# Attention products in four column tiles, denominators from ones, y moved by DMA instead of transposed

## The reference, cut to what matters

```
x = x + 0.5 * ffn0(ln(x));  x = x + attn0(ln(x));  x = x + 0.5 * ffn0(ln(x))
x = x + 0.5 * ffn1(ln(x));  x = x + attn1(ln(x));  x = x + 0.5 * ffn1(ln(x))
# attention: 2 batches, 1024 positions, 512 channels, 16 heads of 32; a0 has 4 key/value heads
att = softmax(where(causal, q k^T / sqrt(32), -inf));  y = att v;  out = y Wo
```

## Time and profile before

| | us |
|---|---|
| median of 3 runs | 2689.49 (2688.24 to 2693.65) |
| the profiled execution | 2691.6 |
| its span, first to last instruction | 2689.9 |
| PE busy | 2610.5 |
| VectorE busy | 1366.2 |
| ScalarE busy | 1081.1 |
| GpSimd busy | 638.1 |

### The profile page before, as it was taken

How to read it: one execution, slowest core, us unless ns; L and a number is a source line. 1 busy time by engine, 2 the same in 40 slices (tenths; PEclk the granted TensorE clock), 3 DMA queues, 4 the chain that set the end, 5 groups by cost and what they waited for, 6 DMA issues and landing times.

```text
span 2689.9 us, 36139 instructions
## 1 busy us (share of the span) xinstructions
PE 2610.5 (97%) x13216; PEld 1994.4 (74%) x13216; DVE 1366.2 (51%) x2784; ACT 1081.1 (40%) x1989; POOL 638.1 (24%) x1102
## 2 busy tenths in 40 slices
PE   6999999999999999999999999999999999999999
PEld 4788765666558888888888888666766678888887
DVE  7787566756655445433333344566366553333333
ACT  7555355655663223311121133666456631111121
POOL 3333532332223335311111130222122321111110
PEclk9999999999999999999999999999999999999999
DMA  4222121122120110100000002332122100000001
GB/s 145 71 71 75 52 52 33 37 56 49 39 86 1 36 44 9 39 25 24 24 24 24 24 24 58 78 80 60 37 66 68 42 24 28 28 24 24 24 16 63
DMA packets 59679, 119.80 MB, mean 45 GB/s; under 512 B 11632, under 2 KB 12656, under 8 KB 59504
## 3 DMA queue, kind: packets, MB, share of 16 engines
q1 hardware_dynamic: 59504, 117.51, 15.4%
HBM read 62.42 MB, written 13.63 MB: 28 GB/s over the span
## 4 chain that ended last, share of the span: by engine, by line
PE 84%; DVE 2%; ACT 2%; issue 2%; DMA 2%; POOL 1%; SPq 1%; DVEq 0%; ACTq 0%; POOLq 0%
PE psum L970 63%; PE psum L1091 9%; PE psum L1055 5%; PE psum L1073 4%; PE psum L979 1%; DMA raw<-in_o 1%; SPq L1644 1%; PE psum L1101 1%; PE psum L1111 1%; ACT s1a0e L1265 0%; ACT s4a1e L1265 0%; POOL rstd L1531 0%; POOL wmem L1543 0%; DVE s4a1masked L1440 0%; DMA raw<-in_q 0%
## 5 line engine op out<-in xcount | busy, mean ns | idle before, releaser
L970 PE MATMUL psum<-hA_hi,wmem 128*128 128x256 f32 (+1 forms) x1536 | 405.4, 334 | 0.1
L970 PE MATMUL psum<-hA_lo,wmem 128*128 128x512 f32 (+1 forms) x864 | 293.7, 340 | 0.0
L970 PEld LDWEIGHTS psum<-hA_hi,wmem 128*128 128x128 f32 x1536 | 270.0, 190 | 30.9 <-DVE wmem L1345 0.5
L1265 ACT ACTIVATE s4a1e<-psum,p_scale 128x384 f32<-128x384 f32 (+5 forms) x384 | 205.4, 581 | 99.1 <-PE psum L1073 96.7
L1265 ACT ACTIVATE s1a0e<-psum,p_scale 128x384 f32<-128x384 f32 (+5 forms) x384 | 205.1, 579 | 95.4 <-PE psum L1073 93.4
L1440 DVE CUSTOM_DVE_ANT_0 s4a1masked<-psum,mask_q 128x512 bf16<-128x512 f32 (+7 forms) x256 | 190.0, 751 | 90.3 <-PE psum L1055 89.1
L1392 DVE SCALAR_TENSOR_TENSOR x<-psum,x 128x512 f32<-128x512 f32 x256 | 175.6, 689 | 97.7 <-PE psum L970 93.4
L1440 DVE CUSTOM_DVE_ANT_0 s1a0masked<-psum,mask_q 128x512 bf16<-128x512 f32 (+7 forms) x256 | 189.1, 751 | 62.5 <-PE psum L1055 59.9
L1363 DVE TENSOR_TENSOR s5f1prod<-psum,s5f1silu 128x512 f32<-128x512 f32 x64 | 44.2, 691 | 314.5 <-PE psum L970 314.5
L1363 DVE TENSOR_TENSOR s3f1prod<-psum,s3f1silu 128x512 f32<-128x512 f32 x64 | 44.2, 691 | 294.5 <-PE psum L970 294.5
L970 PE MATMUL psum<-s3f1w,s3f1a 128*128 128x512 f32 x768 | 181.8, 391 | 0.9 <-POOL s3f1w L1543 0.9
(11 more groups left out here) (196 smaller groups left out, 5054.7 us busy)
## 6 DMA issues: line engine op xcount, KB each, us to landing
s1a0qst<-s1a0qs SPq DMA_DIRECT2D x96, 128.0 KB, 2.4
s4a1qst<-s4a1qs SPq DMA_DIRECT2D x96, 128.0 KB, 2.4
s4a1kst<-s4a1ks SPq DMA_DIRECT2D x96, 128.0 KB, 2.4
raw<-in_gate SPq DMA_DIRECT2D x44, 256.0 KB, 2.8
raw<-in_up SPq DMA_DIRECT2D x44, 256.0 KB, 2.7
raw<-in_down SPq DMA_DIRECT2D x44, 256.0 KB, 2.8
rounded<-s0f0w SPq DMA_DIRECT2D x24, 256.0 KB, 2.0
s2f0w<-rounded SPq DMA_DIRECT2D x24, 256.0 KB, 5.1
```

What stands on the lines that cost most here:

```text
L970: ins = pe.matmul(out_, w, m, start=n == 0, stop=n == len(terms) - 1)
L1265: act.activation(T[s]["e32"][:, begin_ + z * pw:begin_ + (z + 1) * pw - skip], src, ACT.Exp, bias=p_scale[:]).then_inc(sem["exp"], 1)
```

## The change

- `pv` cuts the queries of each 128-block in four quarters of 32 (QUAD = 256 columns per quarter) and sends them to four column tiles of 32 partitions. The value block is 32 columns, without the ones. Columns 0 to 255 of the bank hold y^T of a head.
- After each odd unit GpSimd adds the exponentials of the odd key block onto those of the even one in place (`e_add`). `den` multiplies this sum with a block of ones, in the same four tiles, to columns 256 to 511, so the denominator stands in all 32 rows of a quarter. As the even block now holds the sum, the odd value block is replaced by its difference from the even one (`v_out` on VectorE, `v_dif`).
- `y_fin` takes the reciprocal of 128 x 256 denominators and multiplies the 128 x 256 of y^T with it into `ysb`; `take`, `y_turn` and `y_tp` are gone. Four DMAs per head (`y_move`) bring the four quarters to the head's 32 partitions of `y`; `y_hi` and `y_lo` split the 1024 columns into high and low parts once per group.
- `piece_out` and `oproj` are cut in two steps each (`piece_lo`, `x_sum`), the second one step later. `row` writes the masked scores over the scores in PSUM; `masked` is gone. PV_LAG becomes 9, `e32` 7680 columns, and some steps start at other units.

```diff
-PV_LAG = 7
+PIECES_AT = 2
+Y_AT = 1
+Y_WAIT = 2
+YT_AT = 2
+O_LAG = 1
+NORMS_FROM = 11
+STACKS_AT = (18, 20, 26, 31)
+PV_LAG = 9
-E32 = 5632
+E32 = 7680
...
         def times_v(n, jt):
+            k = jt // 2
             plan.append(("pv", s, n, jt))
-            if jt == ST - 1:
-                job = [[], [("take", s, n)], [], [], [("y_turn", s, n)], [("y_fin", s, n)]]
+            if jt % 2 == 0:
+                plan.append(("den", s, n, k))
+                return
+            if k == PAIRS - 1:
+                job = [[]] * Y_AT + [[("y_fin", s, n)]] + [[]] * Y_WAIT + [[("y_move", s, n)]]
                 g, j = divmod(n, HPG)
                 if j == HPG - 1:
-                    job += [[("y_tp", s, g, 0)], [("y_tp", s, g, 1)], []]
-                    job += [[("oproj", s, g, t)] for t in range(ST)]
+                    job += [[]] * YT_AT + [[("y_hi", s, g)]] + [[("y_lo", s, g)]] + [[]] * O_LAG
+                    job += [[("oproj", s, g, t)] + [("x_sum", s, g, t - 1)] * (t > 0)
+                            for t in range(ST)] + [[("x_sum", s, g, ST - 1)]]
...
             plan.append(("e_mask", s, n, i))
+            if i % 2:
+                plan.append(("e_add", s, n, i // 2))
...
-                on.wait_ge(sem["exp"], at("exp", "key", s, n, jt, pieces - 1))
-                on.wait_ge(sem["e_mask"], at("e_mask", "e_mask", s, n, jt))
-                for c in range(2):
-                    ins = pe.matmul(psum[c * HALF:c * HALF + VW, bank, jt * HALF:CH],
+                name = ("v_out", "v_dif")[jt % 2]
+                on.wait_ge(sem[name], at(name, "v_out", s, n // HEADS, v_of(s, jt)))
+                on.wait_ge(sem["e_add"], at("e_add", "e_add", s, n, jt // 2))
+                for c in range(HPG):
+                    ins = pe.matmul(psum[c * HD:(c + 1) * HD, bank, jt * HD:QUAD],
                                     v[:, jt, kv, :], e[:, :, c, :], start=jt == 0,
                                     stop=jt == ST - 1, skip_group_check=True)
...
+            def den(s, n, k):
+                bank = banks["pv", s, n, 0][0]
+                on.wait_ge(const, CONSTS)
+                on.wait_ge(sem["e_add"], at("e_add", "e_add", s, n, k))
+                e = quarters(s, n, 2 * k)
+                for c in range(HPG):
+                    ins = pe.matmul(psum[c * HD:(c + 1) * HD, bank, QUAD + 2 * k * HD:CH],
+                                    ones[:], e[:, :, c, :], start=False,
+                                    stop=k == PAIRS - 1, skip_group_check=True)
+                ins.then_inc(sem["den"], 1)
...
             def y_fin(s, n):
+                bank, rden = banks["pv", s, n, 0][0], T[s]["rden"][n % 2]
+                on.wait_ge(sem["pv"], at("pv", "pv", s, n, ST - 1))
+                dve.reciprocal(rden[:], psum[:, bank, QUAD:CH]).then_inc(sem["y_rec"], 1)
+                if n >= 2:
+                    on.wait_ge(*y_moved(s, n - 2))
                 on.wait_ge(sem["y_rec"], at("y_rec", "y_fin", s, n))
+                dve.tensor_tensor(T[s]["ysb"][n % 2][:], psum[:, bank, 0:QUAD], rden[:],
                                   ALU.mult).then_inc(sem["y_fin"], 1)
...
+            def e_add(s, n, k):
+                begin, end = e32_place[s, n, 2 * k]
+                more, more_end = e32_place[s, n, 2 * k + 1]
+                _, _, pieces, _ = key_cols(2 * k + 1)
+                e32 = T[s]["e32"]
+                on.wait_ge(sem["exp"], at("exp", "key", s, n, 2 * k + 1, pieces - 1))
+                on.wait_ge(sem["e_mask"], at("e_mask", "e_mask", s, n, 2 * k + 1))
+                pool.tensor_tensor(e32[:, begin + P:end], e32[:, begin + P:end],
+                                   e32[:, more:more_end], ALU.add).then_inc(sem["e_add"], 1)
...
+            def y_move(s, n):
+                g, j = divmod(n, HPG)
+                on.wait_ge(sem["y_fin"], at("y_fin", "y_fin", s, n))
+                if g:
+                    on.wait_ge(sem["y_lo"], at("y_lo", "y_lo", s, g - 1))
+                for c in range(HPG):
+                    sp.dma_start(T[s]["y"][j * HD:(j + 1) * HD, c * QUAD:(c + 1) * QUAD],
+                                 T[s]["ysb"][n % 2][c * HD:(c + 1) * HD, :]
+                                 ).then_inc(moved[n % 2], 16)
```

More of the change, by code:

```diff
@@ L376 @@
     "gu": ("gate", "up", "silu", "prod", "a_hi"), "a_lo": ("a_lo",),
-    "k_ones": ("k_ones",), "v_ones": ("v_ones",),
+    "k_ones": ("k_ones",),
     "piece": ("proj",), "v_tile": ("v_mm",), "v_chunk": ("v_mm", "v_bias"), "v_turn": ("v_tp",),
-    "v_out": ("v_out",), "bias_x": ("x_pool",),
+    "bias_x": ("x_pool",),
     "row": ("s_q", "row_max"), "m_tp": ("m_tp", "m_hi"), "m_lo": ("m_lo",),
-    "key": ("s_k", "exp"), "e_mask": ("e_mask",), "pv": ("pv",), "take": ("y_take",), "y_turn": ("y_turn",),
-    "y_fin": ("y_rec", "y_fin"),
-    "y_tp": ("y_tp", "y_hi", "y_lo"), "oproj": ("o_proj", "x_add"),
+    "key": ("s_k", "exp"), "e_mask": ("e_mask",), "pv": ("pv",),
+    "e_add": ("e_add",), "den": ("den",), "y_fin": ("y_rec", "y_fin"),
+    "y_hi": ("y_hi",), "y_lo": ("y_lo",), "oproj": ("o_proj",), "x_sum": ("x_add",),
 }
@@ L419 @@
 FIT = 1
-EMPTIED_BY = {"piece": "piece_out", "v_tile": "v_out", "v_turn": "v_out", "m_tp": "m_lo",
-              "y_turn": "y_fin", "ln_tp": "ln_lo"}
+EMPTIED_BY = {"piece": "piece_lo", "oproj": "x_sum", "v_tile": "v_out", "v_turn": "v_out", "m_tp": "m_lo",
+              "ln_tp": "ln_lo"}
 def banks_wanted(step):
@@ L567, in bank_turns @@
             if step[0] == "pv":
-                release["take", step[1], step[2]] = mine
+                release["y_fin", step[1], step[2]] = mine
             elif step[0] in EMPTIED_BY:
@@ L917, in read_by @@
                 return sem["m_lo"], at("m_lo", "m_lo", *step[1:])
-            name = {"gu": "prod", "row": "row_max", "key": "exp", "v_chunk": "v_bias",
-                    "y_tp": "y_lo", "oproj": "x_add"}.get(kind)
+            name = {"gu": "prod", "row": "row_max", "key": "exp", "v_chunk": "v_bias"}.get(kind)
             if kind == "down":
@@ L1123, in tensor_program @@
                      "v_chunk": v_chunk, "v_turn": v_turn, "row": row, "m_tp": m_tp, "key": key,
[L1124 removed]
+                     "pv": pv, "den": den, "oproj": oproj}
             for kind, *where in plan:
@@ L1479, in oproj, with x_sum @@
-            def oproj(s, g, t):
+                on.wait_ge(sem["y_hi"], at("y_hi", "y_hi", s, g))
+                dve.tensor_tensor(by_quarter(lo), quarters_of(T[s]["y"]),
+                                  by_quarter(hi).bitcast(F32), ALU.subtract).then_inc(sem["y_lo"], 1)
+            def x_sum(s, g, t):
                 tile = g // HPG * ST + t
@@ L1494, in vector_program @@
                      "q8": q8_, "q_b": q_b, "gu": gu, "a_lo": a_lo, "down": down,
-                     "piece_out": piece_out, "row": row, "m_lo": m_lo,
-                     "y_fin": y_fin, "y_tp": y_tp, "oproj": oproj}
+                     "piece_out": piece_out, "row": row, "m_lo": m_lo, "v_out": v_out,
+                     "y_fin": y_fin, "y_lo": y_lo, "x_sum": x_sum, "piece_lo": piece_lo}
             for kind, *where in plan:
```

258 lines of the change are left out of this document (129 added, 129 removed).

## The result

2648.5 us (median of 4 runs, 2646.1 to 2651.6) against 2690.4 us: ratio 0.9844, 95% interval 0.9827 to 0.9861, 42 us faster. The forecast was 2638 us, range 2598 to 2688. Another execution of the same kernel can differ by 5 us (0.2%). The profiled execution took 2646.1 us (before 2691.6), its span is 2644.4 (before 2689.9): 45.5 us less.

A forecast was written before the change was run, and what follows sets the result against it. PE, busy 97% of the span, was taken as the bound. From the profiled 2691.6 us, 78 less for PE work, plus 22 for waits and 4 for SyncE, gave 2639.6; median 2638 us, range 2598 to 2688.

The forecast's parts named there:

- Products: Attention products on PE: four column tiles overlap fourfold, 0.417 ns per query column, gaining 0.77 us per head.
- Rivals A and E: Four column tiles run only two at a time (2801 us, 10%), or overlap incompletely (2664 us, 5%).
- Transposes: PE in the attention stages: `y_turn` and `y_tp` go, together 0.46 us per head.
- The failed step: PE's idle share in the attention stages rises from 3.8% to 6.5% with VectorE that full: plus 22 us.
- its reciprocal: VectorE's reciprocal of 128x256 takes 1.4 us, between 0.42 and 2.1: plus 1.2 us per head.
- the PSUM writes: Row maxima written over the scores in PSUM cost VectorE 0 to 0.66 us per head; 0 taken.
- rival B: VectorE becomes the bound through slow reciprocal, PSUM writes and waits for GpSimd: 2677 us, 17%.
- "hidden" of GpSimd: GpSimd's `e_add` sums, 5.2 us per head, stay hidden because `pv` is issued 9 blocks behind its last exponential.
- the exclusion of VectorE and GpSimd: VectorE's two-SBUF-input instructions and GpSimd's SBUF reads exclude each other, costing VectorE some 24 us, partly inside the 22.
- "4 us" of SyncE: Four `y_move` DMAs a head delay stacks and `m_lo` in SyncE's queue: 4 us in all, between 0 and 16.
- The prediction's sign: In the attention stages, key products waiting for the DMAs of the maxima would show the prediction wrong.
- Outside: Outside the two attention stages nothing may move.

The follow-up runs named there:

- e2: The changed kernel without GpSimd's sums: plain values, and ones times all eight key blocks: 2685.6 us, 0.9968.
- e1: The changed kernel with the reciprocal taken of only 32 of 256 denominator columns, repeated in the product: 2644.1 us, 0.9826.
- e3: The changed kernel with the row maxima's elementwise output written to SBUF again and a strip of exponentials of 6912 columns: 2645.6 us, 0.9826.
- e5: The changed kernel with two units more between a layer norm tile's statistics and its normalisation in the attention stages: 2636.0 us, 0.9787.
- e11: The changed kernel with y moved by eight DMAs of 128 columns a head instead of four of 256: 2707.5 us, 1.0052.
- e12: The kernel of e5 with two units more between the load of a weight piece and its split in the attention stages: 2634.4 us, 0.9779.
- e8: The changed kernel with the earlier kernel's lag of 7 units and strip of 5632 columns: 2693.7 us, 1.0000.
- e7: The changed kernel with one product with values a unit instead of two every second unit: 2716.5 us, 1.0089.
- e9: The kernel of e5 with four products with values every fourth unit instead of two every second, strip 7936 columns: 2663.9 us, 0.9894.
- e10: As e9, but at the other place of the head, strip 7680 columns, youngest product 6 units old: 2704.8 us, 1.0050.
- e4: The changed kernel with the reciprocal made on ScalarE as exp(-ln) instead of on VectorE: 2853.1 us, 1.0603.

## Why the prediction was right, and where not

- **Products.** Right, and they are the larger part of the gain: 1.38 us for the first pair (forecast 1.4), 0.417 ns a column, confirmed by e2's 0.41. Rivals A and E are out. The Trainium skill (TensorE: Matmul & The Clock Gate, Measured speedup vs the span model) has 2.38 times for three column tiles; here the slope of four is that of a fourfold overlap, half of the twofold one before.
- **Transposes.** Their rows are gone. With both, PE was to shed 78 us; it shed 71.1 in busy time, 86 if the half clock is taken out. The 8 more are not assigned: busy time merges modelled ends.
- **The failed step: "PE idles 13.5 of 360 us now, 3.8%; I take 6.5% with DVE that full, plus 22 us".** The number came out, 21.4 us, the cause did not: the agreement is luck. VectorE's load was as forecast in the first stage (80%; 73% in the second), its reciprocal half way to the upper bound (1.75 us for 1.4 taken, 2.1 the end) and the PSUM writes near their upper end (0.6 us a head for 0 taken). Yet e1 took most of the reciprocal away and e3 the writes, and the waits stayed; that is also why rival B did not come, though VectorE's costs were near its terms. In the lists of waits VectorE's part did not grow (10.7 and 10.4 us). What grew is what ScalarE releases, since it stands in its order: for GpSimd's norm operations, which queue behind a sum (e5 removes them: 12.5 us), and for weights, which SyncE issues behind the moves (e11 doubles that load: +59 us; e12 takes these waits away and gains nothing that can be told).
- **"hidden" of GpSimd.** The sums themselves are hidden: PE waited for them six times, 2.5 us in all, with the long lag and strip. Without these nothing is gained (e8). What was missed is what else stands in GpSimd's order, the norms' small operations: ScalarE waited for 11 and 13 of the 16 tiles of a stage (before: 8 and 7). By e2 some 18 to 22 us went with the sums. For the exclusion of VectorE and GpSimd, which the prediction took from the Trainium skill (SBUF — State Buffer, Who interferes with whom) and put at an estimated 24 us, e2 is the test, as it takes the sums out. `y_lo` (L1519, L1516 in e2) reads two SBUF operands:

```profile
L1519 DVE TENSOR_TENSOR s4a1yT<-s4a1y,s4a1yT x8: 1220/1222/2040, 1708.4 to 2109.4; 128x1024 fp32r<-128x1024 f32 x8
L1516 DVE TENSOR_TENSOR s4a1yT<-s4a1y,s4a1yT x8: 1221/1222/1226, 1726.3 to 2144.3; 128x1024 fp32r<-128x1024 f32 x8
```

  With the sums the longest takes 2040 ns, without them 1226, so the trace agrees with the rule. Its size is small: these and the first stage's `piece_lo` for q are busy for 37.7 us with the sums and 34.5 without: 3 us more.
- **"4 us" of SyncE.** The moves' direct waits are small (`yT` 1.7 and 0.4 us, `m_lo` 1.1 and 1.9, stacks to PE 2.3 and 2.7), and PE's waits for DMAs rose by 4.9 us. The prediction's sign, key products that wait for the DMAs of the maxima, showed twice, 3.0 us. The path through ScalarE's waits for weights was not looked at.
- **Not in the sum: the clock.** +15 us. With it, 2691.6 - 86 + 21 + 15 + 4 = 2645.6 for the profiled 2646.1. This is an account of what was measured and closes by itself: the 86 holds the same 15, and the 4 is the time lost outside the stages, while SyncE's waits lie in the 21. Against the forecast of the profiled execution, 2639.6, it is 8 us less for the products, 5 less for waits (21 for 22 + 4), 15 more for the clock and 4 more outside: 6.5 us. The other 4 of the 10.5 us by which the forecast was low are the step to the median, which was taken as 2.1 us below the profiled execution and lies 2.4 above it. The largest missing term is the clock, and errors of the other sign hid it in part.
- **Outside.** 3.1 us before the first stage, 1.9 between them, 0.8 gained at the end; "nothing may move" was wrong by these, and they were not tested. Before the first stage the clock was halved for 14 us where it was for 7, which can be up to 3 us of it.

## What to carry to other kernels

When work is given to an idle engine or queue, list what else stands in its order and who waits for that: here three 0.2 to 0.6 us operations behind a 1.5 us sum cost 12.5 us, and the 56 us of reciprocals a stage about 5 (e1). Separate a producer and its reader by some more of the plan's units before shortening anything; two empty units gave 12.5 us. A busy share says how much room an engine has, and not whether something waits in its order: the test is to shorten the suspect and see whether the idle time of the bound engine moves.

## What the runs showed of the hardware

- A RECIPROCAL from PSUM costs 150 ns and 6.25 ns an element of a row (349 ns for 128x32, 1750 for 128x256; before, 199 for 128x8); a multiply of 128x256 takes 425.
- The accumulator read behind a row reduction takes 141 ns when the elementwise output goes to PSUM, 82 when it goes to SBUF as bf16.
- Changes between full-width matmuls and 32-column tiles seem to cost TensorE time beyond the columns: 0.26 us a visit by e7, 0.14 by e9, 0.07 by e10. Only e7's is clear of the busy time that moves for other reasons (17 us in e8).
- The granted clock fell to 0.50 behind stretches with gaps in PE's work (the windows above), and a run of matmuls took twice the time at that level. The time at half clock in the two stages, with PE's idle time in them: before 7 and 27 us, e12 17 and 40, e5 24 and 42, changed 37 and 49, e11 102 and 80; but e2 7 with 44 and e9 27 with 78, so idle time alone does not tell it.
- A VectorE subtraction of 128x1024 with two SBUF inputs lasts 1.22 us; beside GpSimd's sums the longest took 2.04, without them (e2) 1.23.
- Exp and Ln in turn load a table, 1283 ns each time (e4).
